# The rows of an expert chunk transposed by SBUF-to-SBUF transfers and VectorE instead of TensorE

## The chip, the cores and the metric

One core of a Trainium2 chip runs the whole program, both stages of it. The metric is the device time of the program in microseconds, as the median of several runs.

## The reference, cut to what matters

A transformer block over 32 sequences of 256 tokens with 512 features: cross-attention with 16 heads, and then a mixture of experts over all 8192 tokens. Only the second part bears on the change:

```python
scores = jax.nn.softmax(xf @ w_gate, axis=-1)
weights, idx = jax.lax.top_k(scores, TOP_K)                # TOP_K = 2 of N_EXP = 8
...                                                        # pos: place of a token in its expert's list
exp_x = exp_x.at[flat_e, pos_c].add(xf[tok] * vmask)       # (8, CAPACITY = 2048, 512)
h = jnp.einsum('ecd,edf->ecf', exp_x, c_fc)                # 512 -> 2 x 768
a, g = jnp.split(h, 2, axis=-1)
h = jax.nn.silu(a) * g
exp_out = jnp.einsum('ecf,efd->ecd', h, c_proj)            # 768 -> 512
out = (exp_out[flat_e, pos_c] * w).reshape(N, TOP_K, d).sum(axis=1)
```

The input of that part is the normalised result of the attention, and its output is added to the residual.

## The kernel before

The first stage, `attention_block`, computes attention and routing, 32 sequences one after the other. It leaves in DRAM the normalised tokens (`xn2_rows`), the residual (`out`) and a table with a list of 2048 slots for each expert. The change doesn't touch it.

The second stage, `expert_block`, takes each expert's 2048 slots in four chunks of 512, so 32 chunks, numbered q. For a chunk, GpSimd gathers 512 rows of 512 values from DRAM into `xg`, which has two buffers: four indirect transfers, one for each 128 rows (L1045). The tokens then stand on the partitions, but the up projection contracts over the features, so these must stand on the partitions. TensorE transposes them in 16 pieces of 128x128 with an identity matrix into PSUM (`turn`, L1187). Four pieces make one group c, 128 features of all 512 tokens, in one of the two banks `turn_ps`. ScalarE rounds the group to a high part `xe_hi` (L1100) and VectorE takes the low part `xe_lo`, the difference (`low`, L1140). The products are made from such pairs in three passes (high by high, high by low, low by high).

The up projection of a chunk has six steps, m from 0 to 5. A step is 24 matmuls of 128x512: 12 for the value half (`a_ps`) and 12 for the gate half (`g_ps`), L1211. Behind a step, ScalarE takes the silu of `a_ps` (L1119), VectorE multiplies it by `g_ps` into `hidden` (L1167), ScalarE rounds that to `ht_hi` (L1124), and VectorE takes `ht_lo` (L1140). `a_ps`, `g_ps`, `act_part` and `hidden` have two buffers each. TensorE begins step m when the product of step m - 2 is done (the semaphore `gated`). The down projection is four groups of 18 matmuls into `y_ps` (L1226); the first of them waits for each `ht_lo` in turn. ScalarE scales its results by the routing weights into `y` (L1133), and GpSimd adds them to `out` in DRAM by indirect transfers, each of which waits until the one before has landed (L1073).

The transposes of chunk q + 1 stand in the steps 2 to 5 of chunk q, one group in front of each step. On ScalarE the rounding of a group comes ahead of the silu of that step. On VectorE the low part of a group comes ahead of the product. The groups of the very first chunk come before everything else, and the first up projection waits for all four. In the first chunk of each expert, ScalarE and VectorE also split the projection weights, a piece `pj_hi` (L1094) and `pj_lo` in each step. In the down projection of an expert's last chunk they split the next expert's `fc_raw`.

SP's queue loads the weights: `load_fc` brings a third of the up projection's weights (1 MB, L994), issued in the middle of the first three chunks of the expert before, and 1.5 MB of `c_proj` in the middle of the fourth (L1017, for the first expert L1002). For the first expert, SP waits until the first chunk is gathered, and then loads the second and third pieces and `c_proj`. SP's waits in the loop are on step counts (`up_done`) and on the splitting of the weights.

GpSimd gathers chunk q + 2 at the beginning of its work for chunk q. It waits until the buffer in `xg` is free, which the semaphore `turned` of the transposes tells.

Inside the attention stage there are 1536 transfers from SBUF to SBUF on SP's queue (`stack_heads`, L281), of 64 KB, from 32 partitions to 32 others.

Of the kernel before, what the change touches and what calls it, by code (L numbers as in the profile page):

```python
# [21 lines left out]
ALU = mybir.AluOpType  # L22
# [3 lines left out]
P = 128  # L26
# [11 lines left out]
CHUNK = 512  # L38
CT = CHUNK // P
CHUNKS = CAPACITY // CHUNK  # L40
AHEAD = 2
# [879 lines left out]
def expert_block(nc, c_fc, c_proj, out, xn2_rows, table):  # L921
    from contextlib import ExitStack
    with ExitStack() as stack:
# [8 lines left out]

        ident = sb("ident2", [P, P])

        fc_raw = sb("fc_raw", [P, DC * 2, GATE])
# [5 lines left out]
        recs = sb("recs", [P, SLOTS, 2], I32)  # L941
        xg = sb("xg", [P, 2, CT, D])
        xt = [sb("xe_hi", [P, 2, DC, CHUNK], F32R), sb("xe_lo", [P, 2, DC, CHUNK], F32R)]
        act_part = sb("act_part", [P, 2, CHUNK])
# [3 lines left out]

        turn_ps = [ps(f"turn_ps{i}", [P, CHUNK]) for i in range(2)]
# [4 lines left out]
        ident_ready = sem("ident_ready")  # L954
        lists_loaded = sem("lists_loaded")
# [8 lines left out]
        gathered = [sem(f"gathered{i}") for i in range(2)]  # L964
        turned = sem("turned2")
        xt_hi_done = sem("xe_hi_done")
# [18 lines left out]
        with nc.Block() as block:  # L985

            @block.sync
            def _(sp):
                sp.dma_start(lists[:, :, :, :], table.rearrange("(e p s) r -> p e s r", p=P, s=SLOTS)).then_inc(
                    lists_loaded, 16)  # L990

                def load_fc(e, j):
                    cols = slice(j * PIECE * P, (j + 1) * PIECE * P)
                    sp.dma_start(fc_raw[:, :, cols], c_fc[e].rearrange(  # L994
                        "p c (h i) -> p (c h) i", h=2)[:, :, cols]).then_inc(fc_loaded[j], 16)

                load_fc(0, 0)

                sp.wait_ge(gathered[0], 16 * CT)
                for j in range(1, PIECES):  # L1000
                    load_fc(0, j)
                sp.dma_start(pj_raw[:, :, :], c_proj[0]).then_inc(pj_loaded, 16)  # L1002
                with sp.Fori(1, EXPERTS) as e:
                    for j in range(PIECES):
                        if j == 0:

                            sp.wait_ge(fc_split, e * MC)
                            settle(sp)

                        sp.wait_ge(up_done, e * (CHUNKS * MC) - (CHUNKS - j) * MC + MC // 2)  # L1010
                        settle(sp)
                        load_fc(e, j)
                    sp.wait_ge(pj_split, e * MC)
                    settle(sp)
                    sp.wait_ge(up_done, e * (CHUNKS * MC) - MC + MC // 2)
                    settle(sp)
                    sp.dma_start(pj_raw[:, :, :], c_proj[e]).then_inc(pj_loaded, 16)  # L1017

            @block.gpsimd
            def _(pool):  # L1020
                nc.gpsimd.memset(ident[:, :], 0.0).then_inc(ident_ready, 1)
                pool.wait_ge(ident_ready, 1)
                nc.gpsimd.affine_select(out=ident[:, :], in_=ident[:, :], compare_op=ALU.not_equal, fill=1.0,
                                        base=0, pattern=[[-1, P]], channel_multiplier=1).then_inc(ident_ready, 1)
                pool.wait_ge(lists_loaded, 16)

                def gather(q, e, i):

                    par = i % 2
                    rows = slice(i * CT, (i + 1) * CT)  # L1030


                    if is_step(e, 0):
                        pass
                    elif i // 2:
                        pool.wait_ge(gathered[par], e * (8 * CT * CHUNKS))
                    else:
                        pool.wait_ge(gathered[par], e * (8 * CT * CHUNKS) - 16 * CT)
                    nc.gpsimd.tensor_copy(gather_ids[:, rows, :], lists[:, e, rows, :]).then_inc(ids_ready, 1)
                    pool.wait_ge(ids_ready, q + 1)  # L1040

                    need(pool, turned, (q - 1) * DC)
                    settle(pool)
                    for t in range(CT):
                        nc.gpsimd.indirect_dma_start(  # L1045
                            out=xg[:, par, t, :], out_offset=None, in_=xn2_rows[:, :],
                            in_offset=bass.IndirectOffsetOnAxis(
                                ap=gather_ids[:, i * CT + t, 0:1].bitcast(U32), axis=0)).then_inc(gathered[par], 16)
# [33 lines left out]
            def _(act):  # L1082
# [13 lines left out]
                def turn(q, par, c):  # L1096

                    need(act, up_done, (q - 1) * MC)
                    act.wait_ge(turned, q * DC + c + 1)
                    nc.scalar.copy(xt[0][:, par, c, :], turn_ps[c % 2][:, :]).then_inc(xt_hi_done, 1)  # L1100

# [36 lines left out]
            def _(dve):  # L1138
# [7 lines left out]

                def turn(q, par, c):
                    dve.wait_ge(xt_hi_done, q * DC + c + 1)
                    low(xt[1][:, par, c, :], turn_ps[c % 2][:, :], xt[0][:, par, c, :], xt_split)

                fc_lo(0, 0)
                for c in range(DC):
                    turn(0, 0, c)
                for m in range(1, MC):
                    fc_lo(0, m)

                def expert(e, final):
                    for i in range(CHUNKS):
                        q = e * CHUNKS + i
                        for m in range(MC):  # L1160
# [8 lines left out]
                            dve.wait_ge(ht_hi_done, q * MC + m + 1)  # L1169
                            low(ht[1][:, m, :], hidden[:, m % 2, :], ht[0][:, m, :], ht_split)  # L1170
                        if i == CHUNKS - 1 and not final:
                            for m in range(MC):
                                fc_lo(e + 1, m)
# [3 lines left out]
            def _(pe):  # L1177
                pe.wait_ge(ident_ready, 2)
# [12 lines left out]
                for c in range(DC):  # L1191
                    turn(0, 0, 0, c)

                def expert(e, final):
                    for i in range(CHUNKS):
                        q = e * CHUNKS + i
                        need(pe, xt_split, q * DC + DC)
                        for m in range(MC):
                            if m >= MC - DC and i < CHUNKS - 1:
                                turn(q + 1, e, i + 1, m - (MC - DC))  # L1200
                            elif m >= MC - DC and not final:
                                turn(q + 1, e + 1, 0, m - (MC - DC))
                            if i == 0:
# [72 lines left out]
```

## Time and profile before

| | |
|---|---|
| median of 3 runs | 3083.16 us (3080.51 to 3084.5) |
| profiled execution | 3081.46 us, of which the span of the profile is 3079.7 us |
| TensorE busy | 2998.1 us, 97% of the span |
| VectorE, ScalarE, GpSimd busy | 1448.5, 1523.5, 1259.1 us |
| expert stage | from about 1416 us to the end |
| VectorE and ScalarE busy in a chunk's 50 us (1473 to 1523) | 10.7 and 11.4 us |

The span is the time from the first to the last recorded instruction; the little around it belongs to the run, not to the trace. TensorE's busy time counts a matmul from its start to its modelled end, and two that follow each other overlap, so for the pace of matmuls the distance of their starts is read. Idle time of an engine that isn't the bottleneck costs nothing.

### The profile page before, as it was taken

To read this page: it belongs to the slowest core of one execution; us is meant where nothing else is said; L and a number is where in the kernel's file an instruction comes from. 1 tells how busy PE (TensorE), PEld (TensorE's weight loads), DVE (VectorE), ACT (ScalarE), POOL (GpSimd) and SP (SyncE) were. 2 spreads that over 40 slices of the span, in tenths; PEclk is the share of its full clock that TensorE was granted. 3 is DMA by queue.
4 is the path that set the end of the run, shared out by engine and by line. 5 is a ranking of instruction groups with operands and counts; after the bars stand their busy time and mean duration, and the time that the engine had idled before them with its cause. 6 is when DMAs were issued, how large, how long until landed. Compare 5 with 4: busy or idle time off the path is not lost.

```text
span 3079.7 us, 55845 instructions
## 1 busy us (share of the span) xinstructions
PE 2998.1 (97%) x18336; PEld 2537.2 (82%) x18336; DVE 1448.5 (47%) x4906; ACT 1523.5 (49%) x3910; POOL 1259.1 (41%) x1913
## 2 busy tenths in 40 slices
PE   6999999999999999995999999999999999999998
PEld 6888888888888888874888888888888888888886
DVE  5777777777777777763223222131232221312321
ACT  4777778777778777772223232232232322322321
POOL 4666666666666667652121222221222222121211
PEclk9999999999999999997999999999999999999999
DMA  5444444444444445433232323232323333333212
GB/s 166 119 130 128 130 123 129 120 125 133 130 122 125 126 122 133 123 82 132 48 82 48 76 56 76 50 81 52 79 52 72 59 72 53 79 54 77 43 27 28
DMA packets 216664, 281.83 MB, mean 92 GB/s; under 512 B 38336, under 2 KB 161216, under 8 KB 214848
## 3 DMA queue, kind: packets, MB, share of 16 engines
q1 hardware_dynamic: 153312, 144.89, 17.6%
q0 software_dynamic: 32768, 67.26, 12.8%
q10 hardware_dynamic: 30304, 66.07, 6.7%
q8 instruction: 161, 2.64, 0.4%
q14 instruction: 119, 0.97, 0.2%
HBM read 109.53 MB, written 67.90 MB: 58 GB/s over the span
## 4 chain that ended last, share of the span: by engine, by line
PE 52%; DMA 1%; issue 0%; POOL 0%; ACT 0%; SPq 0%; DVE 0%; POOLq 0%
PE a_ps L1211 17%; PE g_ps L1211 17%; PE y_ps L1226 17%; PE turn_ps L1187 2%; DMA pj_raw<-in_c_proj 1%; DMA out<-y,recs 0%; DMA xg<-xn_rows,gather_ids 0%; POOL xg L1045 0%; DMA lists<-table 0%; POOL out L1073 0%; ACT L1119 0%; SPq L994 0%; DVE hidden L1167 0%; ACT y L1133 0%; ACT pj_hi L1094 0%
## 5 line engine op out<-in xcount | busy, mean ns | idle before, releaser
L1073 POOL DMA_INDIRECT out<-y,recs x128 | 204.9, 1601 | 1243.3 <-ACT y L1133 926.1
L371 POOL TENSOR_SCALAR probs<-probs,row_inv 128x256 f32<-128x256 f32 x1024 | 489.3, 489 | 418.1 <-DVE row_inv L584 413.7
L1167 DVE TENSOR_TENSOR hidden<-act_part,g_ps 128x512 f32<-128x512 f32 x192 | 132.2, 688 | 1001.5 <-ACT act_part L1119 1001.5
L575 DVE CUSTOM_DVE_ANT_0 probs<-scores_ps,mask_add,row_any 128x256 f32<-128x256 f32 x1024 | 454.8, 481 | 266.7 <-PE scores_ps L791 262.9
L475 ACT ACTIVATE probs<-probs,low 128x256 f32<-128x256 f32 x1024 | 513.9, 504 | 106.6 <-DVE low L575 93.2
L1119 ACT ACTIVATE act_part<-a_ps 128x512 f32<-128x512 f32 x192 | 114.8, 598 | 675.0 <-PE g_ps L1211 675.0
L460 ACT COPY probs_t<-probs_t_ps 128x512 f32<-128x512 f32 x512 | 299.6, 585 | 186.1 <-PE probs_t_ps L803 137.6
L803 PE MATMUL probs_t_ps<-ident,probs 128*128 128x128 f32 x2048 | 310.1, 273 | 7.0 <-POOL probs L371 6.9
L1211 PE MATMUL a_ps<-xe_hi,fc_hi 128*128 128x512 f32 x768 | 312.3, 407 | 4.3 <-DVE hidden L1167 2.9
L1211 PE MATMUL a_ps<-xe_hi,fc_lo 128*128 128x512 f32 x768 | 301.6, 393 | 0.0
L1211 PE MATMUL a_ps<-xe_lo,fc_hi 128*128 128x512 f32 x768 | 300.7, 392 | 0.0
L1211 PE MATMUL g_ps<-xe_hi,fc_lo 128*128 128x512 f32 x768 | 299.3, 390 | 0.0
L1211 PE MATMUL g_ps<-xe_hi,fc_hi 128*128 128x512 f32 x768 | 299.1, 389 | 0.0
L1226 PE MATMUL y_ps<-pj_lo,ht_hi 128*128 128x512 f32 x768 | 299.0, 389 | 0.0
L1226 PE MATMUL y_ps<-pj_hi,ht_hi 128*128 128x512 f32 x768 | 299.0, 389 | 0.0
L1211 PE MATMUL g_ps<-xe_lo,fc_hi 128*128 128x512 f32 x768 | 299.0, 389 | 0.0
L1226 PE MATMUL y_ps<-pj_hi,ht_lo 128*128 128x512 f32 x768 | 299.0, 389 | 0.0
L1133 ACT ACTIVATE y<-y_ps,recs 128x512 f32<-128x512 f32 x128 | 88.3, 689 | 353.2 <-PE y_ps L1226 332.9
L803 PEld LDWEIGHTS probs_t_ps<-ident,probs 128*128 128x128 f32 x2048 | 238.5, 140 | 9.2 <-POOL probs L371 9.2
L791 PE MATMUL scores_ps<-k_stack,q_stack 96*128 96x256 f32 x1024 | 208.4, 286 | 3.5 <-DMA q_stack<-qk_lo 2.2
L791 PEld LDWEIGHTS scores_ps<-k_stack,q_stack 96*128 96x128 f32 x1024 | 176.4, 191 | 26.8 <-DMA q_stack<-qk_lo 3.0
L1140 DVE TENSOR_TENSOR ht_lo<-hidden,ht_hi 128x512 fp32r<-128x512 f32 x192 | 133.1, 693 | 132.2 <-ACT ht_hi L1124 132.2
(167 smaller groups left out, 6612.4 us busy)
## 6 DMA issues: line engine op xcount, KB each, us to landing
k_stack<-qk_hi SPq DMA_DIRECT2D x512, 64.0 KB, 2.0
q_stack<-qk_hi SPq DMA_DIRECT2D x512, 64.0 KB, 2.9
fc_raw<-in_c_fc SPq DMA_DIRECT2D x24, 1024.0 KB, 5.7
k_stack<-qk_lo SPq DMA_DIRECT2D x256, 64.0 KB, 2.0
q_stack<-qk_lo SPq DMA_DIRECT2D x256, 64.0 KB, 2.9
out<-x_xn ACTq DMA_DIRECT2D x32, 512.0 KB, 3.3
xn_rows<-x_xn ACTq DMA_DIRECT2D x32, 512.0 KB, 3.7
cin<-in_ctx_t ACTq DMA_DIRECT2D x31, 512.0 KB, 4.1
```

Source lines behind the costliest of these rows:

```text
L371: last = nc.gpsimd.tensor_scalar(probs[:, r, t, :], probs[:, r, t, :], row_inv[:, r, t:t + 1], 1.0, ALU.mult, ALU.mult)
L460: nc.scalar.copy(probs_t[:, turned_slot(h)], probs_t_ps[h % 2][:, :, :]).then_inc(turned_copied, 1)
L475: last = nc.scalar.activation(probs[:, s % 4, t, :], probs[:, s % 4, t, :], ACT.Exp, scale=-1.0, bias=low[:, s % 4, t:t + 1], accum_out=ro ...
L575: last = nc.vector.tensor_tensor_reduce(out=probs[:, s % 4, t, :], in0=scores_ps[s % 2][:, t, :], in1=mask_add[:, t, :], scale=row_any[:, ...
L791: last = nc.tensor.matmul(scores_ps[s % 2][:, t, :], stacks[0][:, s // HPC, s % HPC, t * P:(t + 1) * P], stacks[1][:, s // HPC, s % HPC, : ...
L803: last = nc.tensor.transpose(probs_t_ps[h % 2][:, u, t * P:(t + 1) * P], probs[:, h % 4, t, u * P:(u + 1) * P], ident[:, :])
L1073: nc.gpsimd.indirect_dma_start(out=out[:, :], out_offset=bass.IndirectOffsetOnAxis(ap=recs[:, i * CT + t, 0:1].bitcast(U32), axis=0), in_= ...
L1119: nc.scalar.activation(act_part[:, m % 2, :], a_ps[m % 2][:, :], ACT.Silu).then_inc(silu_done, 1)
L1140: nc.vector.tensor_tensor(dst, source, hi.bitcast(F32), ALU.subtract).then_inc(done, 1)
L1167: nc.vector.tensor_tensor(hidden[:, m % 2, :], act_part[:, m % 2, :], g_ps[m % 2][:, :], ALU.mult).then_inc(gated, 1)
L1211: last = nc.tensor.matmul(bank[:, :], fc[a][:, c * 2 + half, m * P:(m + 1) * P], xt[b][:, i % 2, c, :], start=first, stop=(c == DC - 1 and ...
L1226: last = nc.tensor.matmul(y_ps[t % 2][:, :], ht[a][:, m, t * P:(t + 1) * P], pj[b][:, m, :], start=first, stop=(m == MC - 1 and (a, b) == ...
```

## The change

The 16 transposes of a chunk leave TensorE, and with them the identity matrix and the two PSUM banks. In their place stand two steps. SP lays the gathered rows out in quarters (`quarter`): 16 transfers from SBUF to SBUF, each from 32 partitions of `xg` to 32 partitions of the new tile `x_quarters`, 4 runs of 128 values on each partition, 64 KB together. VectorE then transposes `x_quarters` in blocks of 32x32, four instructions of 128x512 for a chunk, into the SBUF tile `x_turned` (for the first chunk of all into four different buffers). ScalarE and VectorE split from there as before. Since the blocks put the features on the partitions in another order, the host lays out `c_fc` to match.

The order on VectorE is now: the transpose of a group ahead of the product of its step, and the subtraction `turn_lo` behind `ht_lo` of the same step. SP's loop is unrolled over all chunks. The transfers for chunk q + 1 stand in SP's queue ahead of the weight load in the middle of chunk q, wait for the gather of that chunk and for the transposes of the chunk before it, and there is one buffer `x_quarters`. GpSimd's gather waits for `quartered` where it waited for `turned`.

```diff
+        x_quarters = sb("x_quarters", [P, CT, GROUPS, P])
+        x_turned = sb("x_turned", [P, CHUNK])
...
+        def x_turn(later, c):
+            return (x_turned[:, :], hidden[:, 0, :], hidden[:, 1, :], act_part[:, 0, :])[0 if later else c]
...
+                def quarter(q):
+                    e, i = divmod(q, CHUNKS)
+                    sp.wait_ge(gathered[i % 2], e * (8 * CT * CHUNKS) + 16 * CT * (i // 2 + 1))
+                    need(sp, x_turned_done, q * DC)
+                    settle(sp)
+                    for j in range(GROUPS):
+                        for a in range(GROUPS):
+                            sp.dma_start(x_quarters[a * DK:(a + 1) * DK, :, j, :],
+                                         xg[j * DK:(j + 1) * DK, i % 2, :, a * P:(a + 1) * P]).then_inc(quartered, 16)
                 load_fc(0, 0)
-                sp.wait_ge(gathered[0], 16 * CT)
+                quarter(0)
                 for j in range(1, PIECES):
                     load_fc(0, j)
                 sp.dma_start(pj_raw[:, :, :], c_proj[0]).then_inc(pj_loaded, 16)
-                with sp.Fori(1, EXPERTS) as e:
...
+                for q in range(EXPERTS * CHUNKS - 1):
+                    quarter(q + 1)
+                    e, i = divmod(q, CHUNKS)
+                    if e + 1 < EXPERTS:
+                        if i < PIECES:
+                            sp.wait_ge(fc_split, (e + 1) * MC)
+                        else:
+                            sp.wait_ge(pj_split, (e + 1) * MC)
+                        sp.wait_ge(up_done, q * MC + MC // 2)
+                        settle(sp)
...
                 def gather(q, e, i):
-                    need(pool, turned, (q - 1) * DC)
+                    need(pool, quartered, (q - 1) * QUARTERED)
...
                 def turn(q, par, c):                     # ScalarE
-                    act.wait_ge(turned, q * DC + c + 1)
-                    nc.scalar.copy(xt[0][:, par, c, :], turn_ps[c % 2][:, :]).then_inc(xt_hi_done, 1)
+                    act.wait_ge(x_turned_done, q * DC + c + 1)
+                    nc.scalar.copy(xt[0][:, par, c, :], x_turn(0 if is_step(q, 0) else 1, c)).then_inc(xt_hi_done, 1)
...
                 def turn(q, par, c):                     # VectorE
+                    if c == 0:
+                        dve.wait_ge(quartered, q * QUARTERED + QUARTERED)
+                    if not is_step(q, 0):
+                        dve.wait_ge(xt_split, q * DC + c)
+                    nc.vector.transpose(x_turn(0 if is_step(q, 0) else 1, c).rearrange("p (g l) -> p g l", l=DK),
+                                        x_quarters[:, :, :, c * DK:(c + 1) * DK].rearrange(
+                                            "p t j l -> p (t j) l")).then_inc(x_turned_done, 1)
+
+                def turn_lo(q, par, c):
                     dve.wait_ge(xt_hi_done, q * DC + c + 1)
-                    low(xt[1][:, par, c, :], turn_ps[c % 2][:, :], xt[0][:, par, c, :], xt_split)
+                    low(xt[1][:, par, c, :], x_turn(0 if is_step(q, 0) else 1, c), xt[0][:, par, c, :], xt_split)
...
                             low(ht[1][:, m, :], hidden[:, m % 2, :], ht[0][:, m, :], ht_split)
+                            if m >= MC - DC and (i < CHUNKS - 1 or not final):
+                                turn_lo(q + 1, (i + 1) % 2, m - (MC - DC))
...
-                def turn(q, e, i, c):                    # TensorE
-                    if c == 0:
-                        pe.wait_ge(gathered[i % 2], e * (8 * CT * CHUNKS) + 16 * CT * (i // 2 + 1))
-                    need(pe, xt_split, q * DC + c - 1)
-                    for t in range(CT):
-                        last = nc.tensor.transpose(turn_ps[c % 2][:, t * P:(t + 1) * P],
-                                                   xg[:, i % 2, t, c * P:(c + 1) * P], ident[:, :])
-                    last.then_inc(turned, 1)
```

## Rows read from the trace of the kernel before

**Rows 1.** The page's busy times: engine, us (share of the span), instructions.

```profile
PE 2998.1 (97%) x18336; PEld 2537.2 (82%) x18336; DVE 1448.5 (47%) x4906; ACT 1523.5 (49%) x3910; POOL 1259.1 (41%) x1913
```

**Rows 2.** The chain of the expert stage, its longest pieces: start us, us, what.

```profile
1428.11 15.70 DMA pj_raw<-in_c_proj
...
1879.71 16.32 PE y_ps L1226 x72
1930.60 16.32 PE y_ps L1226 x72
```

**Rows 3.** Window of one chunk, instructions on turn_ps: busy (count), clock, DMA share, GB/s.

```profile
core 0: us, PE busy (x) PEld busy (x) DVE busy (x) ACT busy (x), PEclk, DMA share, GB/s
...
1879.71:1930.60 50.89, 2.39 (x16) 1.98 (x16) 2.73 (x4) 2.32 (x4) 1.00 0.31 62
```

**Rows 4.** TensorE in order of time: start us, us, engine, line, operation.

```profile
1703.26 0.48 PE L1211 MATMUL a_ps<-xe_hi,fc_hi 128*128 128x512 f32 x1
...
1709.19 0.48 PE L1211 MATMUL a_ps<-xe_hi,fc_hi 128*128 128x512 f32 x1
...
1729.99 0.39 PE L1226 MATMUL y_ps<-pj_hi,ht_hi 128*128 128x512 f32 x1
...
1742.91 0.39 PE L1211 MATMUL a_ps<-xe_hi,fc_hi 128*128 128x512 f32 x1
...
1748.35 0.39 PE L1211 MATMUL a_ps<-xe_hi,fc_hi 128*128 128x512 f32 x1
```

**Rows 5.** VectorE's groups by shape: busy us, mean ns, idle before and its releasers.

```profile
L575 DVE CUSTOM_DVE_ANT_0 probs<-scores_ps,mask_add,row_any 128x256 f32<-128x256 f32 x1024 | 454.8, 481 | 266.7 <-PE scores_ps L791 262.9 <-issue 1.2 <-PE probs_t_ps L803 0.6
```

**Rows 6.** ScalarE in order of time, one step: silu and high part.

```profile
1703.10 0.60 ACT L1119 ACTIVATE act_part<-a_ps 128x512 f32<-128x512 f32 x1 [3.40 <-PE g_ps L1211]
1704.45 0.62 ACT L1124 CAST ht_hi<-hidden 128x512 fp32r<-128x512 f32 x1 [0.75 <-DVE hidden L1167]
```

**Rows 7.** VectorE in order of time: the same step, and step 5's low part.

```profile
1703.73 0.69 DVE L1167 TENSOR_TENSOR hidden<-act_part,g_ps 128x512 f32<-128x512 f32 x1 [3.30 <-ACT act_part L1119]
1705.11 0.69 DVE L1140 TENSOR_TENSOR ht_lo<-hidden,ht_hi 128x512 fp32r<-128x512 f32 x1 [0.69 <-ACT ht_hi L1124]
1705.72 0.68 DVE L1140 TENSOR_TENSOR xe_lo<-turn_ps,xe_hi 128x512 fp32r<-128x512 f32 x1
...
1728.80 0.69 DVE L1140 TENSOR_TENSOR ht_lo<-hidden,ht_hi 128x512 fp32r<-128x512 f32 x1 [0.69 <-ACT ht_hi L1124]
```

**Rows 8.** VectorE in the first chunk of an expert: the weights' low part.

```profile
1858.67 0.68 DVE L1140 TENSOR_TENSOR pj_lo<-pj_raw,pj_hi 128x512 fp32r<-128x512 f32 x1
```

**Rows 9.** The page's DMA issues: count, KB each, median us from issue to landing.

```profile
k_stack<-qk_hi SPq DMA_DIRECT2D x512, 64.0 KB, 2.0
...
xg<-xn_rows,gather_ids POOLq DMA_INDIRECT x128, 3.7
```

**Rows 10.** SP's issues in the attention stage, in order of time.

```profile
703.64 1.24 SPq L281 DMA_DIRECT2D q_stack<-qk_hi  x2
```

**Rows 11.** All transfers of line 281.

```profile
DMA to landing us min/median/max: 2.0/2.4/4.4
```

**Rows 12.** GpSimd in one chunk: the first scatter-add, the last gather.

```profile
1885.61 1.62 POOL L1073 DMA_INDIRECT out<-y,recs  x1 [25.21 <-ACT y L1133]
...
1909.17 1.30 POOL L1045 DMA_INDIRECT xg<-xn_rows,gather_ids  x1 [0.30 <-issue]
```

**Rows 13.** TensorE at the start of the expert stage, in order of time.

```profile
1426.88 1.94 PE L1187 MATMUL turn_ps<-ident,xg 128*128 128x128 f32 x8 [22.13 <-DMA xg<-xn_rows,gather_ids]
...
1432.71 0.50 PE L1211 MATMUL a_ps<-xe_hi,fc_hi 128*128 128x512 f32 x1 [1.40 <-DVE xe_lo L1140]
...
1447.23 0.47 PE L1211 MATMUL a_ps<-xe_hi,fc_hi 128*128 128x512 f32 x1 [2.90 <-DVE hidden L1167]
```

**Rows 14.** Windows at the start of the expert stage; PEclk is the third number from the end.

```profile
core 0: us, PE busy (x) PEld busy (x) DVE busy (x) ACT busy (x) POOL busy (x), PEclk, DMA share, GB/s
...
1429.00:1431.00 2.00, 1.63 (x8) 1.43 (x8) 1.01 (x2) 0.92 (x2) 1.14 (x2) 0.50 0.97 318
...
1448.00:1450.00 2.00, 2.00 (x7) 1.58 (x6) 1.66 (x3) 1.06 (x3) 0.00 (x0) 0.55 0.04 8
1450.00:1452.00 2.00, 2.00 (x7) 1.59 (x6) 1.66 (x3) 1.31 (x3) 0.00 (x0) 0.59 0.00 0
```

More of the change, by code:

```diff
@@ L39 @@
 CT = CHUNK // P
+GROUPS = P // DK
+QUARTERED = 16 * GROUPS * GROUPS
 CHUNKS = CAPACITY // CHUNK
@@ L931, in sem @@
             return stack.enter_context(nc.semaphore(name))
-        ident = sb("ident2", [P, P])
         fc_raw = sb("fc_raw", [P, DC * 2, GATE])
@@ L947, in expert_block @@
         y = sb("y", [P, CT, D])
-        turn_ps = [ps(f"turn_ps{i}", [P, CHUNK]) for i in range(2)]
+        def x_turn(later, c):
+            return (x_turned[:, :], hidden[:, 0, :], hidden[:, 1, :], act_part[:, 0, :])[0 if later else c]
         a_ps = [ps(f"a_ps{i}", [P, CHUNK]) for i in range(2)]
@@ L952, in expert_block @@
         y_ps = [ps(f"y_ps{i}", [P, D]) for i in range(2)]
-        ident_ready = sem("ident_ready")
         lists_loaded = sem("lists_loaded")
@@ L964, in expert_block @@
         gathered = [sem(f"gathered{i}") for i in range(2)]
-        turned = sem("turned2")
+        quartered = sem("quartered")
+        x_turned_done = sem("x_turned_done")
         xt_hi_done = sem("xe_hi_done")
@@ L1002, in _ @@
                 sp.dma_start(pj_raw[:, :, :], c_proj[0]).then_inc(pj_loaded, 16)
-                with sp.Fori(1, EXPERTS) as e:
[L1004 to L1010, printed above, removed]
-                        settle(sp)
[L1012 to L1017, printed above, removed]
+                for q in range(EXPERTS * CHUNKS - 1):
[7 more added lines that the diff above has]
+                        sp.wait_ge(up_done, q * MC + MC // 2)
+                        settle(sp)
+                        if i < PIECES:
+                            load_fc(e + 1, i)
+                        else:
+                            sp.dma_start(pj_raw[:, :, :], c_proj[e + 1]).then_inc(pj_loaded, 16)
             @block.gpsimd
             def _(pool):
[L1021 to L1024, printed above, removed]
                 pool.wait_ge(lists_loaded, 16)
@@ L1153, in _ @@
                     turn(0, 0, c)
+                    if c:
+                        turn_lo(0, 0, c - 1)
+                turn_lo(0, 0, DC - 1)
                 for m in range(1, MC):
@@ L1177, in _ @@
             def _(pe):
-                pe.wait_ge(ident_ready, 2)
-                def turn(q, e, i, c):
-                    if c == 0:
-                        pe.wait_ge(gathered[i % 2], e * (8 * CT * CHUNKS) + 16 * CT * (i // 2 + 1))
-                    need(pe, xt_split, q * DC + c - 1)
-                    for t in range(CT):
-                        last = nc.tensor.transpose(turn_ps[c % 2][:, t * P:(t + 1) * P],
-                                                   xg[:, i % 2, t, c * P:(c + 1) * P], ident[:, :])
-                    last.then_inc(turned, 1)
-                for c in range(DC):
-                    turn(0, 0, 0, c)
                 def expert(e, final):
@@ L1198, in expert @@
                         for m in range(MC):
[L1199 to L1202, printed above, removed]
                             if i == 0:
@@ L1264 @@
         "w_gate": rows_to_partitions(got["L0_ffn_w_gate"], DC),
-        "c_fc": rows_to_partitions(got["L0_ffn_c_fc"], DC),
+        "c_fc": np.ascontiguousarray(got["L0_ffn_c_fc"].reshape(EXPERTS, GROUPS, DC, P // GROUPS, DFF).swapaxes(
+            2, 3).reshape(EXPERTS, P, DC, DFF)),
         "c_proj": rows_to_partitions(got["L0_ffn_c_proj"], MC),
```

## The prediction

> **What bounds the kernel now.** I read the shares and the clock first, then the chain, then one chunk of the expert stage by engine, then the start of that stage, because the change touches nothing else. The page has TensorE busy for 97% of the span [rows 1], and a chunk of the expert stage has it at a granted clock of 1.00 [rows 3], which is 2.4 GHz. The expert stage runs from about 1416 us to the end. In the chain two down projections in a row start 1930.60 - 1879.71 = 50.89 us apart, each 16.32 us of 72 matmuls, without a wait between [rows 2]. A chunk is 6 steps of 24 matmuls and 72 more, 216 in all, so 0.2267 us each (16.32 / 72), or 48.96 us. What is left, 1.93 us, is the transposes: 16 of them, four in front of each of steps 2 to 5, which the window of one chunk books as 2.39 us of overlapping busy time [rows 3]. The pitch of the steps says it directly: with transposes 1703.26 to 1709.19 = 5.93 us, without 1742.91 to 1748.35 = 5.44 us, so 0.49 us for four and 1.96 us a chunk [rows 4]. VectorE and ScalarE sit idle for over half of a chunk. TensorE alone sets the pace here, except in the first 30 us of the stage.
>
> **TensorE's part, removed.** 31 chunks carry the transposes of the next one: 31 x 1.94 (between 1.93 and 1.96) = **-60.1 us**. This is also the most that can be won, because the first chunk's four groups stand in the start, worked out below. The identity matrix built on GpSimd goes too, but GpSimd then waits for the lists anyway, so that is nothing.
>
> **VectorE's part, added.** Four transposes of 128x512 per chunk. The trace shows none. From below it could be half of a plain operation, 0.35 us, for it reads one input and not two; the nearest rows are the plain 128x512 f32 operations at 0.69 us [rows 7], and from above the 128x256 operation of 481 ns with more in it, which doubled is 0.96 us [rows 5]. I take 0.7 us, a plain pass. What hides it is VectorE's idle time in a step. Follow one cycle from ScalarE's silu to the next, by its starts: silu 1703.10, product 1703.73, high part 1704.45, low part 1705.11, the x low part 1705.72 [rows 6, 7]. The last one is held up by nobody, and ends 0.68 later, at 3.30 us after the silu. Then come the transpose T and ScalarE's copy of it (0.62, as the high part), and some 0.1 for the semaphores: 4.02 + T, and the next silu is due after 5.44 us. So T is free up to **1.4 us**. In the first chunk of an expert the low part of the projection weights stands in that cycle too, another 0.61 us by the distance of two such starts (1705.11 to 1705.72) [rows 7, 8], and T is free up to **0.8 us**. What is late next if T is longer: silu, then step 5's low part, which the down projection needs. That one ends at 1728.80 + 0.69 = 1729.49, and its reader, the 16th matmul, starts at 1729.99 [rows 4, 7]: 0.5 us of slack. Lag adds up over steps 3, 4 and 5. With T = 0.7 there is none; with 0.96 it is 3 x 0.16 = 0.48 us, within the slack. Cost 0 for both bounds. ScalarE's copies and VectorE's subtractions now read SBUF where they read PSUM; the rows of both kinds lie within 0.04 us of each other, nothing.
>
> The Trainium skill (VectorE: DVE Perf Modes, The three transpose paths) has 311 ns for a 128x128 bf16 transpose on VectorE, and its Rules for kernel authors send a 128x128 transpose to TensorE where PSUM will do as the destination, which speaks against this change. An estimate from it is 4 x 311 = 1.24 us per instruction: 3 x 0.44 - 0.5 = 0.8 us in each of 8 first chunks, and the sum would be some 6.5 us higher. No row of before shows which.
>
> **The SBUF-to-SBUF transfers, added.** 16 per chunk of 64 KB on SP's queue. The nearest rows are the stacking transfers of the attention stage, the same size between the same kinds of place: 1.24 us for two of 0.60, so one every 0.64 us, and 2.0 us (the median over both kinds 2.4) from issue to landing [rows 9 to 11]. So 16 x 0.64 = 10.2 us of issue and 2.0 to 2.4 us behind the last: about 12.5 us a chunk. The new ones have runs of 512 B, the old ones 1 KB; half as long, so from below it may be no different, and from above I take the longest landing of any of the 1536, 4.4 us [rows 11], for the last one: 12.2 to 14.6 us. In the steady state they are hidden. They may start once the last transpose of the chunk before has read the buffer, in step 5, about 31.2 us into the chunk (five steps 27.2, and 3.3 + T into the sixth); they end at 44. Their first reader stands in front of step 2's product in the next chunk, which has to be met at 48.96 + 16.3 - 1.3 = 64.0 us. Slack 20 us. Queued behind them on SP are only the weight loads, which wait for the middle of the next chunk anyway. Queued behind the reader on VectorE are the products, and TensorE waits for those, which is why the slack matters. The gathers on GpSimd, which SP now waits for, are issued by 1910.5 us and land 3.7 us later [rows 9, 12], at 1914.2, in a chunk that began where the down projection before it ended, at 1879.71 + 16.32 = 1896.03 [rows 2]: 18 us into the chunk, 13 us before SP asks for them. The transfers fall beside the scatter-adds of the down projection, but GpSimd stands idle for 25.2 us ahead of the first of these in a chunk [rows 12]; a slower scatter is absorbed. No transfers run in the last chunk, so the tail is as before. Cost 0.
>
> **The start of the stage, moved.** Nothing covers it here. Before: the first rows are there at 1426.88, TensorE transposes, and the first up projection starts at 1432.71 [rows 13]. After: SP issues 16 transfers, 10.2 us, the last lands 2.0 later, at 1438.5 or so; then VectorE runs four transposes between four subtractions, T, T, low, T, low, T, low and low = 4 x 0.65 + 4 x 0.65 + some waiting for ScalarE = 5.6 us. TensorE starts at 1444.1, 11.4 us later. But before, it soon stood still again: 2.90 us ahead of 1447.23 [rows 13]. By the chain that is the load of the projection weights, 15.70 us from 1428.11 to 1443.81 [rows 2], which ScalarE rounds ahead of its first silu. SP now issues two weight pieces and this load behind the 16 transfers, 10.2 us later. If it takes as long again it lands at 1454.0, and TensorE goes on 3.4 us behind, at 1457.4; if the gathers that ran beside it before are over, some 3 us sooner. TensorE's own two steps end at 1444.1 + 10.9 = 1455.0, or later, because it starts at half clock: the granted clock was 0.50, its level of 1.2 GHz, still from 1429 to 1431, when the transposes had run since 1426.88, and it dipped to 0.55 and 0.59 in the 4 us from 1448, behind the 2.9 us of standing still: 4 x 0.43 = 1.7 us lost [rows 14]. At 1.2 GHz for 4 us it is 2 us late, 1457.0. So it goes on between 1455 and 1457.5 where it did at 1447.23, and the dip may be gone. From +6 to +10.3, and up to +14 if the second chunk's transfers, which queue behind the projection load, come after step 2. I take **+9 us**.
>
> **The sum.** Profiled execution: span 3079.7 - 60.1 + 9 = 3028.6, and 1.76 around it (3081.46 - 3079.7) make 3030.4. The median of the runs is 3083.16, 1.7 above the profiled one, so **3032 us**, 1.66% faster. By the ends (transposes -59.8 to -60.8, start +6 to +14, lag 0) 3028 to 3038; with 4 us for the spread of the runs (3080.51 to 3084.5) 3024 to 3042.
>
> The Trainium skill (DMA: Bandwidth & Descriptors, Bandwidth) gives 0.95 us for a 64 KB transfer and calls transfers under 64 KB dominated by descriptors. By it the 16 would take 15.2 us instead of 10.2, and the start and the sum are 5 us longer; the trace's pitch of 0.64 us is on the other side.
>
> **Rivals.**
> - *Slow transposes* (the other sign). If T is well above 1.4 us, every chunk lags: 23 chunks by 3(T - 1.4) - 0.5, 8 by 3(T - 0.8) - 0.5. Together 93T - 131 us; it eats the 51 us at T = **1.96 us**. At 2.2 us it is 73 us, so 3032 + 73 = **3105 us**, slower by 0.7%. For it: no transpose in the trace, and 32x32 blocks with 4-byte values could go at a quarter of the usual rate (0.69 x 4 = 2.76). Against: each VectorE row of 128x512 lies at 0.69 or below.
> - *Between*: T from 1.2 to 1.9, or a start of +14 and more: **3042 to 3076 us**.
> - *Late transfers*: they eat the slack if their pitch is (64.0 - 31.2 - 2.9) / 16 = 1.87 us or more. At 2.2 us it is 5.3 us for each of 30 chunks, **3190 us**. For it: the spread of the landings up to 4.4 us, where one waits behind others [rows 11]. Against: the pitch of 0.64 in a stage with busier queues [rows 10].
> - *The change gives TensorE nothing*: another wait keeps the pitch at 50.89 us. Then only the start is left, 3083 + 9 = **3092 us**. For it: the 0.5 us of slack ahead of the down projection. Against: nothing in that path grows.
>
> **Chances.** Forecast 3024 to 3042: 0.76. Between: 0.10. Slow transposes 0.06, late transfers 0.03, nothing for TensorE 0.02; some 0.03 between the last ones and no change. A change of under 0.2% (6.2 us) is what a measurement here can't tell from none. Faster 0.86, same 0.04, slower 0.10. The range 3024 to 3052 leaves out the rivals' 0.11, half of the between case and a little below, under 2 in 10.
>
> **What would show it.** Right: no transposes on TensorE; down projections 48.96 us apart; a_ps steps of 5.44 us throughout; transposes on VectorE near 0.7 us; 16 transfers every 0.64 us that end before the chunk's down projection does; TensorE's first up projection near 1444 and its next standing still over by 1458. Wrong: VectorE's transposes above 1.4 us, an idle row of TensorE in front of the down projection released by the low part, VectorE waiting for a transfer in step 2 of any chunk but the first, or a granted clock below 1 in the steady chunks.

## The result and the profile after

The changed kernel takes 3030.13 us (median of 4 runs, 3029.69 to 3035.1) against 3083.83 (4 runs): ratio 0.9833, 95% interval 0.9821 to 0.9845. Run again later on another chip (the tenth experiment) it has 0.9843 (0.983 to 0.9857), 3030.89 us. So it is 1.6 to 1.7% faster, 48 to 52 us by the ratios and 50 to 54 by the medians; 3032 was forecast. The profiled execution is the slowest of its runs, 3035.1 us, 4.2 above the tenth experiment's. Most of that lies ahead of the expert stage, which alone the change touches: the lists' load is issued at 1420.07, where it was 1415.90 in the profile of before and 1416.44 in the tenth experiment. Times of the expert stage are therefore compared from the first chunk's gather on.

The chain of the expert stage, its longest pieces, which answer to [rows 2]:

```profile
1532.36 16.32 PE y_ps L1234 x72
...
2071.43 16.32 PE y_ps L1234 x72
2120.39 16.32 PE y_ps L1234 x72
...
2953.45 16.32 PE y_ps L1234 x72
```

The kernel before has, with the same number of chunks between them:

```profile
1523.18 16.32 PE y_ps L1226 x72
...
2999.87 16.32 PE y_ps L1226 x72
```

In the changed kernel two down projections in a row are 48.96 us apart, the time of the 216 matmuls, and up to 0.4 us more where a new expert begins. Over 29 chunks (1532.36 to 2953.45) the mean is 49.00 us; before it was 50.92 (1523.18 to 2999.87). A window of one chunk, all instructions (columns as in [rows 14]):

```profile
2071.43:2120.39 48.96, 48.96 (x217) 40.54 (x217) 13.45 (x20) 12.56 (x20) 10.43 (x9) 1.00 0.40 86
```

In this window TensorE never waits and its granted clock is 1.00, and from the first down projection to the end the trace has no wait of its matmuls for another engine. VectorE is busy for 13.5 us of 49, where it was 10.7 of 51; the DMA engines' share went from 0.31 to 0.40. The new instructions by the tiles they touch (duration min/median/max in ns), and the landing of the transfers:

```profile
L1012 SPq DMA_DIRECT2D x_quarters<-xg x512: 585/601/1829, 1431.1 to 2913.4; - x171
L1166 DVE STREAM_TRANSPOSE x_turned<-x_quarters x125: 698/711/712, 1443.0 to 2951.4; 128x512 f32<-128x512 f32 x125
...
DMA to landing us min/median/max: 2.0/2.0/10.2
```

The first row is the issues, 0.6 us each. A transpose takes 0.71 us. In a step it stands where it was meant to, and ScalarE is the engine to look at for the room left, in order of time (an ordinary chunk first, then an expert's first chunk):

```profile
1520.21 0.62 ACT L1113 CAST xe_hi<-x_turned 128x512 fp32r<-128x512 f32 x1 [2.16 <-DVE x_turned L1166]
1521.51 0.60 ACT L1132 ACTIVATE act_part<-a_ps 128x512 f32<-128x512 f32 x1 [0.68 <-PE g_ps L1219]
```

```profile
1471.67 0.62 ACT L1113 CAST xe_hi<-x_turned 128x512 fp32r<-128x512 f32 x1 [2.06 <-DVE x_turned L1166]
1472.55 0.60 ACT L1132 ACTIVATE act_part<-a_ps 128x512 f32<-128x512 f32 x1 [0.26 <-PE g_ps L1219]
```

The silu still waits for TensorE and not for the transpose, with 0.68 us to spare, and 0.26 where the projection weights are split too. The start of the stage, SP and VectorE in order of time:

```profile
1431.11 10.38 SPq L1012 DMA_DIRECT2D x_quarters<-xg  x16
1441.53 1.31 SPq L1000 DMA_DIRECT2D fc_raw<-in_c_fc  x2
1442.89 1.73 SPq L1019 DMA_DIRECT2D pj_raw<-in_c_proj  x1
```

```profile
1442.98 0.71 DVE L1166 STREAM_TRANSPOSE x_turned<-x_quarters 128x512 f32<-128x512 f32 x1 [13.69 <-DMA x_quarters<-xg]
```

and TensorE, which answers to [rows 13]:

```profile
1448.32 0.79 PE L1219 MATMUL a_ps<-xe_hi,fc_hi 128*128 128x512 f32 x1 [39.41 <-DVE xe_lo L1153]
...
1452.33 0.63 PE L1219 MATMUL a_ps<-xe_hi,fc_hi 128*128 128x512 f32 x1
...
1453.06 0.39 PE L1219 MATMUL a_ps<-xe_hi,fc_lo 128*128 128x512 f32 x1
...
1461.47 0.39 PE L1219 MATMUL a_ps<-xe_hi,fc_hi 128*128 128x512 f32 x1
```

The 16 transfers take 10.38 us to issue, the last lands 11.9 us behind the gather (1431.11 to 1442.98), and the first matmul comes 17.2 us behind it, where it was 5.8 before. It starts at half clock, 1.2 GHz (matmuls 0.43 us apart until 1452.75), and then runs without a pause. Step 2 begins at 1461.47, 30.4 us behind the gather; before it was 20.35 (1447.23 - 1426.88). From the gather to the second down projection it is 101.25 us (1532.36 - 1431.11), and was 96.30. Before, 3.9 us of that were the transposes in these two chunks, which are gone: the start costs 101.25 - (96.30 - 3.9) = 8.9 us. With the steady part, 31 x (50.92 - 49.00) = 59.5, the change is worth 50.6 us.

### The profile page after: what moved, and what is told of

It is laid out like the page before. It is cut to its first block, busy times and chain, and to the rows that moved or that the text cites. A ratio compares the mean times of both kernels' runs of the same rounds, so it can differ in the third digit from the quotient of the medians.

```text
span 3033.3 us, 55379 instructions
## 1 busy us (share of the span) xinstructions
PE 2938.5 (97%) x17824; PEld 2489.2 (82%) x17824; DVE 1533.9 (51%) x5034; ACT 1542.7 (51%) x3910; POOL 1262.6 (42%) x1911
## 3 DMA queue, kind: packets, MB, share of 16 engines
q1 hardware_dynamic: 227040, 178.48, 22.5%
## 4 chain that ended last, share of the span: by engine, by line
PE 51%; DMA 1%; SPq 0%; issue 0%; POOL 0%; DVE 0%; ACT 0%; POOLq 0%
PE a_ps L1219 17%; PE g_ps L1219 17%; PE y_ps L1234 17%; DMA out<-y,recs 0%; SPq L1012 0%; DMA xg<-xn_rows,gather_ids 0%; POOL xg L1058 0%; DMA lists<-table 0%; DMA x_quarters<-xg 0%; DVE xe_lo L1153 0%; POOL out L1086 0%; ACT xe_hi L1113 0%; DVE x_turned L1166 0%; ACT y L1146 0%; DVE act_part L1166 0%
## 5 line engine op out<-in xcount | busy, mean ns | idle before, releaser
L1219 PE MATMUL a_ps<-xe_hi,fc_hi 128*128 128x512 f32 x768 | 300.3, 391 | 39.7 <-DVE xe_lo L1153 39.4
L1113 ACT CAST xe_hi<-x_turned 128x512 fp32r<-128x512 f32 x125 | 77.6, 621 | 255.5 <-DVE x_turned L1166 255.5
L1219 PEld LDWEIGHTS a_ps<-xe_hi,fc_hi 128*128 128x128 f32 x768 | 144.6, 188 | 71.1 <-DVE xe_lo L1153 39.5
```

The costliest lines, as they stand in the source:

```text
L1219: last = nc.tensor.matmul(bank[:, :], fc[a][:, c * 2 + half, m * P:(m + 1) * P], xt[b][:, i % 2, c, :], start=first, stop=(c == DC - 1 and ...
```

## The experiments

Each time stands beside runs of the kernel before on the same chip, whose medians lie between 3080.14 and 3080.88 us.

**1. The first chunk on TensorE, the rest as changed.** The 16 transposes of the first chunk come back with the identity matrix and two PSUM banks. The feature order is 4p + c on both ways. The waits on semaphores that count the first chunk's transfers and transposes are moved to match (not shown).

```diff
-                quarter(0)
+                sp.wait_ge(gathered[0], 16 * CT)
...
+                for c in range(DC):                      # TensorE, ahead of the first expert
+                    need(pe, xt_split, c - 1)
+                    for t in range(CT):
+                        last = nc.tensor.transpose(turn_ps[c % 2][:, t * P:(t + 1) * P],
+                            xg[:, 0, t, :].rearrange("p (i k) -> p k i", k=DC)[:, c, :], ident[:, :])
+                    last.then_inc(turned, 1)
...
-    x_quarters[:, :, :, c * DK:(c + 1) * DK].rearrange("p t j l -> p (t j) l")
+    x_quarters.rearrange("p t j (l k) -> p k (t j) l", k=DC)[:, c, :, :]
```

> The changed kernel, but the very first chunk is transposed on TensorE as before, and nothing but chunks 1 to 31 goes over the quarters and VectorE. The blocks and the weights use the feature order 4p + c so that both ways give the same layout; VectorE then reads with a step of 4 values. Theory (the gain is TensorE's 31 x 1.94 us, less a start that costs 9): the start is as before, first up projection 5.8 us behind the first gather, and the whole gains about 9 us on the changed kernel: 3022 us, ratio to before 0.980. Rival (the start costs nothing, the steady part gains less than 60): no faster than the changed kernel, 3030 us. If VectorE's read with a step costs more, its transposes are above 0.71 us in the trace.

Measured: 3019.71 us, ratio 0.9804 (0.9791 to 0.9818). This version beats both kernels: 9.9 us below the second experiment, which starts like the changed kernel and ran on the same chip, and 11 us below the changed kernel in the tenth, on another one. The first up projection comes 5.9 us behind the gather (1431.66 to 1437.55), as before, and the second down projection 90.9 us behind it (1431.66 to 1522.51), 10.4 us sooner than in the changed kernel. The start's cost is thus real, and avoidable. The reading step showed too (duration min/median/max in ns):

```profile
L1181 DVE STREAM_TRANSPOSE x_turned<-x_quarters x124: 1071/1081/1092, 1455.8 to 2941.1; 128x512 f32<-128x512 f32 x124
```

Reading every fourth value raises the transpose from 0.71 to 1.08 us. TensorE's matmuls wait for nobody from 1480 us to the end, so it costs nothing. In an ordinary chunk that was to be expected, with 1.08 below 1.4 us. In an expert's first chunk the prediction's limit of 0.8 would have given 3 x 0.28 - 0.5 = 0.3 us of waiting; the limit that the changed kernel shows is higher, its 0.71 us and the 0.26 to spare, and ScalarE's silu can follow the copy 0.09 us closer than was reckoned (sixth experiment): 1.06 us.

**2. Half of the first chunk's transfers on ScalarE's queue.**

```diff
-                    for j in range(GROUPS):
+                    for j in range(GROUPS // 2 if q == 0 else GROUPS):
...
+                act.wait_ge(gathered[0], 16 * CT)
+                for j in range(GROUPS // 2, GROUPS):
+                    for a in range(GROUPS):
+                        act.dma_start(x_quarters[a * DK:(a + 1) * DK, :, j, :],
+                                      xg[j * DK:(j + 1) * DK, 0, :, a * P:(a + 1) * P]).then_inc(quartered, 16)
```

> The changed kernel, but 8 of the first chunk's 16 transfers are issued by ScalarE's queue, which is idle then, beside SP's 8. Theory (the start's cost is 16 issues in a row at 0.64 us): the last lands 5.1 us earlier, TensorE starts 5 us earlier, and as the weight loads behind them also go out 5 us earlier, the time falls by 3 to 5 us: 3025 to 3027 us. Rival (the transfers are bound by the DMA engines, not by the issue): the transfers end no earlier than 10 us behind their start, no change, 3030 us.

Measured: 3029.64 us, ratio 0.9834 (0.9821 to 0.9848); no 3 to 5 us. The issue is over after 6.4 us on the slower of the two queues, but VectorE's first transpose still waits for the last transfer, which lands 10.3 us behind the gather (SP's and VectorE's rows):

```profile
1427.55 5.88 SPq L1012 DMA_DIRECT2D x_quarters<-xg  x8
```

```profile
1437.81 0.71 DVE L1171 STREAM_TRANSPOSE x_turned<-x_quarters 128x512 f32<-128x512 f32 x1 [1.53 <-DMA x_quarters<-xg]
```

So landing is 1.6 us sooner than the 11.9 of the changed kernel, not 5.1: the issue alone doesn't set the start. TensorE starts 15.6 us behind the gather (1443.14), also 1.6 sooner, but the second down projection comes only 0.8 us sooner (1527.97, 100.4 us behind the gather), because the first matmuls stay at 1.2 GHz for 6.1 us here and not 4.4.

**3. The kernel before without its steady transposes.**

```diff
...
                         for m in range(MC):
-                            if m >= MC - DC and i < CHUNKS - 1:
-                                turn(q + 1, e, i + 1, m - (MC - DC))
-                            elif m >= MC - DC and not final:
-                                turn(q + 1, e + 1, 0, m - (MC - DC))
```

ScalarE's wait for `turned` goes too for these chunks, and GpSimd's gather waits for ScalarE's rounding in its place (not shown).

> The kernel before, with TensorE's transposes left out for chunks 1 to 31 (only those of the first chunk run; ScalarE and VectorE split what stands in PSUM, so the expert output is not the reference's). It measures the most that the change can give. Theory: 31 x 1.94 = 60 us below before, 3024 us, ratio 0.9805, chunks 48.96 us apart. Rival (TensorE waits for something else once the transposes are gone): chunks more than 49.5 us apart, 3040 us or more.

Measured: 3020.14 us, ratio 0.9806 (0.9793 to 0.982), 60.0 us below before, with 48.98 us as the mean distance of 29 chunks (1518.60 to 2939.03):

```profile
1518.60 16.32 PE y_ps L1223 x72
...
2939.03 16.32 PE y_ps L1223 x72
```

That is TensorE's whole share, and the first experiment, which computes everything, reaches it.

**4. Every VectorE transpose twice.**

```diff
+                    for other in (hidden, act_part)[:AGAIN] if not is_step(q, 0) else ():   # AGAIN = 1
+                        nc.vector.transpose(other[:, c % 2, :].rearrange("p (g l) -> p g l", l=DK),
+                                            x_quarters[:, :, :, c * DK:(c + 1) * DK].rearrange("p t j l -> p (t j) l"))
```

> The changed kernel with each VectorE transpose of chunks 1 to 31 run twice (the extra result is thrown away), so T = 1.34 instead of 0.71 us. Theory (T is free up to 1.4 us, in an expert's first chunk up to 0.8 to 0.9; 0.5 us of slack ahead of the down projection): no wait in 23 chunks, in 8 chunks 3 x 0.4 to 0.55 - 0.5 = 0.6 to 1.1 us, so 5 to 9 us more: 3035 to 3039 us, with TensorE idle ahead of the down projection of each expert's first chunk only. Rival (VectorE has room for far more, as it is busy for a third of the chunk): no change, 3030 us. Rival (any addition to VectorE costs its time): 124 x 0.63 = 78 us more, 3108 us.

Measured: 3033.86 us, ratio 0.985 (0.9835 to 0.9865). Against the ratios of the changed kernel itself (0.9833 and 0.9843) that is 2 to 5 us more, at or below the lower end of what was expected, for 79 us of added work (124 x 0.64). The intervals overlap, so the time alone doesn't show a cost. The waits do (us in total, times, longest; PEld is TensorE's weight load):

```profile
PEld y_ps L1239 <- DVE ht_lo L1154: 4.2, 8, 0.7
```

Eight waits, ahead of the down projection, for step 5's low part, one in the first chunk of each of the eight experts and none in any other chunk: the place and the count that the slack gives. Their size is smaller than reckoned, some 0.5 us of the weight load each, and the mean distance of 29 chunks grows only from 49.00 to 49.07 us.

**5. Two queues, and SP's weight loads only behind them.**

Added to the edit of the second experiment:

```diff
                 quarter(0)
+                sp.wait_ge(quartered, QUARTERED)
```

> The first chunk's 16 transfers on two queues as in the second experiment, and SP issues its weight loads only when they have landed. Theory (in the second experiment the transfers' issue was done after 6 us, but they landed no earlier than 10 us, because the weight loads issued right behind them on SP took half of the DMA engines): they land 7 to 8.5 us behind the gather, TensorE starts 13 to 14 us behind it instead of 15.6, and the time falls by 2 to 3 us against the second experiment, 3027 us. Rival (16 transfers of 64 KB beside a gather take 10 us of the DMA engines by themselves): landing at 10 us as before, and the weights later still, 3031 us or more.

Measured: 3027.84 us, ratio 0.9831 (0.9818 to 0.9845). The transfers landed 11.0 us behind their start (SP's next load goes out at 1435.77, the first transfer at 1424.73), no sooner:

```profile
1424.73 6.21 SPq L1012 DMA_DIRECT2D x_quarters<-xg  x8
1435.77 1.31 SPq L1000 DMA_DIRECT2D fc_raw<-in_c_fc  x2
```

The weight loads had not been the cause: this theory falls. What filled the DMA engines in the 12 us from 1424 to 1436, by queue (packets, MB, share of 16 engines), is mostly the second chunk's gather, q0, beside the transfers on SP's and ScalarE's queues, q1 and q10:

```profile
q0 software_dynamic: 330, 1.07, 39.1%
q10 hardware_dynamic: 1152, 0.52, 23.4%
q1 hardware_dynamic: 1152, 0.52, 23.2%
```

**6. Every transpose three times** (`AGAIN = 2`).

> The changed kernel with each VectorE transpose of chunks 1 to 31 run three times, T = 1.97 us. Theory by the recorded formula: 93 x 1.97 - 131 = 52 us more, back at the time of before, 3080 us; by the slack measured in the changed kernel (0.68 us in a step, 0.26 in an expert's first chunk) 23 x (3 x 0.6 - 0.5) + 8 x (3 x 1.0 - 0.5) = 50 us, the same. TensorE then waits ahead of every down projection but the last. Rival (the lag doesn't add up from step to step): 0.6 us a chunk, 3050 us.

Measured: 3066.75 us, ratio 0.9955 (0.994 to 0.997), 34 to 38 us above the changed kernel by the ratios and not 50. Three groups of waits of the expert stage:

```profile
PEld y_ps L1239 <- DVE ht_lo L1154: 33.7, 31, 1.8
...
PE y_ps L1239 <- DVE ht_lo L1154: 20.6, 31, 1.4
...
PE y_ps L1239 <- DVE pj_lo L1154: 4.6, 8, 0.6
```

Now 31 down projections wait for `ht_lo`, all but the last, and 8 of them for the low part of the projection weights too. ScalarE's silus of steps 3 and 4 are 5.85 us apart instead of 5.44:

```profile
1569.67 0.59 ACT L1133 ACTIVATE act_part<-a_ps 128x512 f32<-128x512 f32 x1
...
1575.52 0.59 ACT L1133 ACTIVATE act_part<-a_ps 128x512 f32<-128x512 f32 x1
```

The lag adds up over three steps, but by 0.41 us a step and not 0.6: three transposes in a row take 1.9 us from the first start to the last end, not 1.97, and the silu starts 0.53 us behind the start of the copy, not 0.62 and a semaphore. For an ordinary chunk this gives 3 x 0.41 - 0.5 = 0.7 us. The chain has it chunk by chunk, at the place in the down projection where TensorE has waited for `ht_lo`:

```profile
1584.10 13.22 PE y_ps L1239 x57
1633.95 13.24 PE y_ps L1239 x57
1685.30 13.26 PE y_ps L1239 x57
1735.02 13.26 PE y_ps L1239 x57
```

An ordinary chunk takes 49.7 to 49.9 us, so 0.7 to 0.9 more than 48.96, and an expert's first chunk 51.4 to 51.7 (here 1633.95 to 1685.30), so 2.4 to 2.7 more, where the formula had 3 x (1.97 - 0.8) - 0.5 = 3.0. So the lag adds up as the formula has it, and the limit for an ordinary chunk is near 1.9 - 0.41 = 1.5 us and not 1.4.

**7 and 8. The same bytes in more and smaller transfers**: 32 of 32 KB, and 64 of 16 KB, for each chunk but the first.

```diff
+                            for k in range(PARTS if q else 1):                              # PARTS = 2 or 4
+                                ts = slice(k * CT // PARTS, (k + 1) * CT // PARTS) if q else slice(0, CT)
-                            sp.dma_start(x_quarters[a * DK:(a + 1) * DK, :, j, :],
+                                sp.dma_start(x_quarters[a * DK:(a + 1) * DK, ts, j, :],
```

The counts in the waits on `quartered` follow (not shown).

> The same bytes in 32 transfers of 32 KB for each chunk but the first. Theory (a transfer costs SP 0.64 us of issue whatever its size, and there are 20 us of slack): 20.5 us of issue per chunk, done at about 54 of 64 us, no wait on TensorE, 3030 us; only the second chunk's, at the start, may come late, up to 5 us. Rival (the slack is smaller than worked out): VectorE waits for a transfer in step 2 of each chunk, above 3040 us.

> The same bytes in 64 transfers of 16 KB for each chunk but the first. Theory: 41 us of issue from 31.3 us into a chunk end at 74 with the landing, where 64 is the limit; the chunk becomes as long as issue, landing and the steps 2 to 5, about 60 us, so 30 x 11 = 330 us more, 3360 us, and VectorE waits for the transfers in step 2 of every chunk. Rival (the cost goes by bytes, not by their number): no change, 3030 us.

Measured with 32: 3032.74 us, ratio 0.9844 (0.9829 to 0.9859), the same as the 0.9843 of the changed kernel in the tenth experiment. TensorE waits only in the first chunk, 2.3 us in all, as VectorE waits 5.0 us there for the second chunk's transfers; none from 1490 us on. With 64: 3328.19 us, ratio 1.0803 (1.0783 to 1.0822). SP in order of time, then two of the stage's waits:

```profile
2025.62 41.54 SPq L1015 DMA_DIRECT2D x_quarters<-xg  x64
2067.26 0.60 SPq L1001 DMA_DIRECT2D fc_raw<-in_c_fc  x1
2083.11 42.39 SPq L1015 DMA_DIRECT2D x_quarters<-xg  x64
```

```profile
DVE x_turned L1169 <- DMA x_quarters<-xg: 397.5, 32, 24.5
...
PE a_ps L1222 <- DVE hidden L1196: 218.2, 31, 19.7
```

The pitch is 0.65 us for 16 KB as for 64 KB, so the cost of SP's issue goes by the number, and the chunk is 57.5 us long (2083.11 - 2025.62). The issue grew by some 10 us a chunk in the seventh experiment, which was free, and by 31 in the eighth, which costs 57.5 - 49 = 8.5 us a chunk. That bounds the slack between 10 and 31 us and puts it near 31 - 8.5 = 22.5. In the eighth, VectorE's transposes of a chunk are 4.6 us apart and not 5.44 (2011.03, 2015.62, 2020.22, 2024.82), because the value and gate halves that its products wait for are there already; less these 3 x 0.84 us, the estimate is 20.

**9 and 10. The transfers by themselves, and the changed kernel again.** The ninth is the fifth experiment with the second chunk's gather held back too; the tenth has no edit.

```diff
                 gather(0, 0, 0)
+                pool.wait_ge(quartered, QUARTERED)
                 gather(1, 0, 1)
```

> As the fifth experiment, and the gather of the second chunk is issued only when the first chunk's 16 transfers have landed, so these have the DMA engines to themselves. Theory now (in the fifth experiment the transfers landed 11 us behind their start, though all were issued after 6.4, because their packets, 47% of 16 engines over 12 us, and the gather's, 39%, filled the engines together): by themselves they need 5.6 us of the engines and land 7 to 8.5 us behind their start, and TensorE starts 13 to 14 us behind the gather. The time falls by 0 to 3 us against the control, as the weights also come later. Rival (16 such transfers take 11 us by themselves, whatever runs beside them): landing at 11 us again.

> The changed kernel itself, unchanged, on the same chip and beside the same runs of before as the ninth experiment: a ratio of 0.983, 3030 us. It is the measure for the start's experiments, which differ from it by a few us.

Measured: 3028.33 us, ratio 0.9831 (0.9818 to 0.9845), and for the tenth 3030.89, ratio 0.9843 (0.983 to 0.9857). Now the transfers have landed when SP's next load goes out, 7.0 us behind the gather:

```profile
1427.15 5.16 SPq L1012 DMA_DIRECT2D x_quarters<-xg  x8
1434.14 1.31 SPq L1000 DMA_DIRECT2D fc_raw<-in_c_fc  x2
```

TensorE starts 13.1 us behind the gather (1440.22), and 17.2 in the tenth experiment (1444.59 - 1427.36). So beside a gather the 16 transfers land 10 to 11 us behind their start even on two queues, and with the DMA engines to themselves after 7.0. On one queue the issue takes 10.4 us by itself. Taking away the issue's bound alone gained 0.9 to 1.6 us of landing (second and fifth experiments); taking away the gather alone, on one queue, was not run. The second down projection comes 97.9 us behind the gather against 101.4. The medians differ by 2.6 us, and the two intervals overlap, so that the whole kernel is faster by it isn't shown.

## Why the prediction was right

- **TensorE's part**: forecast -60.1 us; third experiment 60.0, in the changed kernel 31 x 1.92 = 59.5. No other wait took its place.
- **VectorE's part**: T forecast 0.7 us, measured 0.71, cost 0. That there is a limit, and where it bites, is shown by the fourth and sixth experiments: the same wait, 8 times and 31 times. The limits were set too low (1.4 us against 1.5 in an ordinary chunk, 0.8 against some 1.06 in an expert's first), so the price of a slow transpose was too high: 50 us for three transposes where 34 to 38 were measured. An estimate from these puts the rival's turning point near 2.05 us and not 1.96 (1.9 us cost about 36, and each further us costs 93). None of this touched the forecast, as 0.71 us lies below every limit. The estimate from the Trainium skill (VectorE: DVE Perf Modes, The three transpose paths), four times 311 ns for 128x512, is not what the trace shows: 0.71 us instead of 1.24. The rule of the Trainium skill (VectorE: DVE Perf Modes, Rules for kernel authors) to transpose 128x128 on TensorE where the result may stand in PSUM didn't hold for this place, as TensorE is the engine that is short; for the first chunk, where TensorE has nothing to do, it did (first experiment).
- **The transfers**: pitch forecast 0.64 us, measured 0.65 (10.38 / 16) at the start and 0.64 to 0.71 later (10.29 and 11.42 us for 16), start 31.35 us into the chunk (1531.06 - 1499.71) where 31.2 was forecast, landing 2.0 us. The estimate of 15.2 us for the 16, which the prediction set beside its own 10.2, isn't what the trace shows. The slack of 20 us agrees with the seventh and eighth experiments. The longest landing, 10.2 us, was over twice the 4.4 taken from the rows. It is one of the second chunk's, issued while 3.5 MB of weights are under way at the start (between 1446 and 1470 us the landings are 2.2 to 10.2 us, with a median of 7.2); it cost TensorE nothing.
- **The start**: forecast +9 us, measured 8.9; TensorE's first matmul 17.2 us behind the gather as forecast, step 2 at 30.4 us where 28 to 30.5 was forecast, half clock for 4.4 us where 4 was taken. TensorE's own pace set step 2 and not the projection load, which was one of the two ways left open; the product that step 2 needs was ready 1.1 us before (1459.69 + 0.69 = 1460.38 against 1461.47). Step 2 itself comes 10.0 us later than before, and 1.1 us of that is won back behind it: the granted clock stays at 1.00 from 1456 us on, while before it dipped to 0.55 and 0.59 just behind step 2's start [rows 14]. The prediction held that possible and priced it at 1.7. That the sum is within 0.1 us is partly luck, for +9 was picked out of +6 to +14. One step of the working left something out: it took the 16 issues as the only bound on the landing. They set it in the changed kernel, where the last transfer lands 2 us behind its issue, but the second, fifth and ninth experiments show a bound almost as high, the DMA engines beside the second chunk's gather.

The two measurements of the changed kernel, 0.9833 and 0.9843, differ by less than their intervals. Why a new expert's first chunk comes up to 0.4 us late, before as after, is open.

## What to carry to other kernels

If one engine sets the pace and the others idle, work that leaves it is worth its pitch there (0.49 us per group of four), not its booked busy time (0.60 us), and the new place has to be followed through one full cycle of the engines that hand work to each other, because the room is in that cycle (0.68 and 0.26 us here) and not in the share of idle time. Price the first round separately: what is hidden in the steady part lies open there, and the better kernel may do the first round the old way, as in the first experiment (3019.71 us). When a wait seems to be set by the issue of transfers, look at the share of the DMA engines in the same window before shortening it.

## What the runs showed of the hardware

- VectorE's 32x32 block transpose of f32, 128x512, takes 0.71 us (median of 125), three in a row 1.9 us together (sixth experiment), and 1.08 us when it reads every fourth value (first experiment, median of 124).
- SP issues SBUF-to-SBUF transfers of 16, 32 and 64 KB at about the same pitch: 64 of 16 KB in 41.54 us, 32 of 32 KB in 20.5 to 22.6, 16 of 64 KB in 10.3 to 11.4 (0.64 to 0.71 us each).
- Sixteen such transfers of 64 KB with runs of 512 B, on two queues, take 47% of the 16 DMA engines over 12 us beside a gather, which is 5.6 us of all 16 (fifth experiment), and 64% over 7.1 us by themselves (1427.1 to 1434.2), which is 4.5 us (ninth).
- Behind 39.4 us without a matmul, the first ones of the expert stage ran at a granted clock of 1.2 GHz for 4.4 us in the changed kernel (from 1448.32 to 1452.75), and behind 37.7 us for 6.1 us in the second experiment (1443.14 to 1449.28).
